# Fused two-layer attention, float32 split in high and low parts: theta written where it is used, only phi copied, and ScalarE's order within a slot

## Chip, cores and metric

The kernel runs on one core of a Trainium2 chip. The metric is the device time of one execution in microseconds (us), the median of the runs.

## What is computed

For each of 32 images x (128 channels by 1024 pixels), two attention layers follow one another:

```
theta = W_theta x + b_theta            # 64 x 1024
phi   = W_phi x + b_phi                # 64 x 1024
x1    = x + W_fuse (x softmax(theta^T phi / 8)^T) + b_fuse
h     = group_norm(x1)
q, k, v = W_q h + b, W_k h + b, W_v h + b
y     = x1 + W_p (v softmax(q^T k / sqrt(128))^T) + b_p
```

All inputs and outputs are float32. To keep float32 precision, the kernel splits an operand into a rounded high part and the rest, the low part, and multiplies the parts separately.

## The kernel before, in words

**Rounds and slots.** The work is a pipeline of rounds, one for each image, and each round has 16 slots. In slot s TensorE makes the scores of tile s (128 queries by 1024 keys): tiles 0 to 7 are layer 1 of the round's own image, tiles 8 to 15 layer 2 of the image before it. The loops over slots are written out in the program (`body`, one in each engine's block), and a hardware loop repeats a round. Every engine works through its own fixed list: within a slot, functions are called in the order in which `body` names them, and an instruction that waits holds up all that stands behind it on the same engine.

**A tile's way.** TensorE writes the scores into one of three parts of `s_ps` in PSUM (`scores`, line 452). VectorE takes the row maximum (`maxima`, L750), ScalarE the exponential (`exponentials`, L649). Of four tiles, the first is "copied" (exponential into `e_copied` in SBUF, high part by ScalarE at L672, low part by GpSimd), two are "crossed" (high part by ScalarE in `pair_hi`, L674, low part by VectorE in `take_lo`, L767) and one is "turned" (TensorE transposes it, L487, in the slot behind its own; ScalarE takes the high part at L659, VectorE the low at L761). Copied and crossed tiles are transposed by DMA (SyncE's queue, L368). TensorE multiplies the transposed tiles with the values (`values`) from six slots later on. Before TensorE writes scores into a part of PSUM again, it waits until the tile that was there has been read; for a crossed tile that is `take_lo`.

**Units.** Small products share the slots: `UNITS` says which is made in which slot (theta and phi of the next image, tp0 and tp1 for the two halves of its pixels, in slots 10 and 12; v0 in slot 14, v1 in slot 2; k0, k1, q0, q1, w0, w1 for layer 2; gn1 and gn2 for the group norm; mx for a bound). TensorE makes the unit behind the slot's scores; ScalarE brings it to one of the buffers of `stage` (`take_unit`); GpSimd splits it into high and low (`split_units`, L889 and L892) a slot or two later. ScalarE waits until the unit that had the stage buffer before has been split.

**Theta and phi.** W_theta and W_phi stand side by side, so tp0 and tp1 have theta in partitions 0 to 63 and phi in 64 to 127. The product of layer 1 wants theta's high part in partitions 0 to 63 of `theta2` and its low part in 64 to 127, and phi's high and low parts, each twice, in both halves of the partitions of `phi2`. Before, GpSimd wrote the two parts to `tp_hl`, and in slot 13 SyncE copied them with four DMAs once all had been split:

```
sp.dma_start(phi2[0:D, :, :].bitcast(F32), phi_hl).then_inc(s_tp_copy, 16)
sp.dma_start(phi2[D:C, :, :].bitcast(F32), phi_hl).then_inc(s_tp_copy, 16)
sp.dma_start(theta2[0:D, :].bitcast(F32), theta_hl[:, 0, :]).then_inc(s_tp_copy, 16)
sp.dma_start(theta2[D:C, :].bitcast(F32), theta_hl[:, 1, :]).then_inc(s_tp_copy, 16)
```

They are lines 425 to 428. At slot 0 of the next round TensorE waits for all four: `pe.wait_ge(s_tp_copy, 16 * TP_COPIES * before(mx_at, it, 0))`.

**ScalarE's slot, before:** `turned_hi`, `exponentials`, `pair_hi`, `take_unit`, `inputs_hi`. **VectorE's slot, before:** `take_bounds`, `maxima`, `normalised`, `take_lo`, `reciprocals`, `bound_to_scale`, `x_maxima`, `statistics`.

Of the kernel before, what the change touches and what calls it, by code (L numbers as in the profile page):

```python
# [7 lines left out]
F32 = mybir.dt.float32  # L8
F32R = mybir.dt.float32r
# [5 lines left out]
C = 128  # L15
# [37 lines left out]

UNITS = {0: "gn1", 1: "gn2", 2: "v1", 4: "k0", 5: "k1", 6: "q0", 7: "w0", 8: "q1", 9: "mx", 10: "tp0", 11: "w1",
         12: "tp1", 14: "v0"}
STAGE = {"v1": 0, "k0": 1, "k1": 0, "q0": 1, "w0": 0, "q1": 1, "tp0": 0, "w1": 1, "tp1": 0, "v0": 1}

SPLIT_LAG = {"v1": 2, "k0": 1, "k1": 1, "q0": 1, "w0": 1, "q1": 1, "tp0": 1, "w1": 1, "tp1": 1, "v0": 1}
STAGES = 2
XR_SLOT = 0  # L60
XS_SLOT = 1
X_MAX_SLOT = 7
MX_SLOT = 9
X_SLOT = 8
X_LO_SLOTS = (9, 11)
H_SLOT = 2
H_LO_SLOTS = (3, 4)
RES_SLOTS = (5, 12)
TP_COPY_SLOT = 13
TP_COPIES = 4  # L70

INS = ["x", "w_theta_t", "w_phi_t", "w_fuse_t", "q_w_t", "k_w_t", "p_w_t", "v_w", "vectors", "ident",
       "group_avg"]
# [7 lines left out]
def attention_pair(nc: bass.Bass, x, w_theta_t, w_phi_t, w_fuse_t, q_w_t, k_w_t, p_w_t, v_w, vectors,  # L81
# [88 lines left out]
    def until_stage_before(it, s):  # L170
# [4 lines left out]
                         if staged_at(p) and STAGE[UNITS[p % SLOTS]] == STAGE[UNITS[s]]), -SLOTS - 1)  # L175
        return value(lambda i: count(staged_at, 0, last(i) + 1), it)

    def place(s):

        return PAIRS - 1 if s % GROUP == COPIED and s // GROUP % 2 else s % GROUP  # L180
# [24 lines left out]
    with ExitStack() as ctx:  # L205
# [30 lines left out]
        h_hi, h_lo = sb("h_hi", [C, N], F16), sb("h_lo", [C, N], F16)  # L236
        theta2 = sb("theta2", [C, N], F32R)
        phi2 = sb("phi2", [C, 2, N], F32R)

        tp_hl = sb("tp_hl", [C, 2, N], F32R)  # L240
        q_hi, q_lo = sb("q_hi", [C, N], F32R), sb("q_lo", [C, N], F32R)
        k_hi, k_lo = sb("k_hi", [C, N], F32R), sb("k_lo", [C, N], F32R)
        v_hi = [sb(f"v_hi{n}", [P, KB, C], F16) for n in range(2)]
# [70 lines left out]
        s_clamped = [sem(f"bound_clamped{n}") for n in range(4)]  # L314
        s_scale = [sem(f"value_scale_ready{n}") for n in range(4)]
        s_den = sem("den_scaled_ready")
        s_tp_copy = sem("theta_phi_copied")
        s_split_hi = sem("unit_split_hi")
        s_split = sem("unit_split")
        s_xhi = sem("x_hi_ready")  # L320
# [21 lines left out]
        @block.sync  # L342
        def _(sp):
            sp.dma_start(xs[:, :], x[0]).then_inc(s_xs, 16)
            for dst, src in LOADS0:
                sp.dma_start(dst, src).then_inc(s_wload0, 16)
            for dst, src in LOADS:
                sp.dma_start(dst, src).then_inc(s_wload, 16)

            def batch(t, b):  # L350
                return t[b] if isinstance(b, int) else t[bass.ds(b, 1)].rearrange("a c n -> c (a n)")

            def transposes(it, s):
                if here(crossed_at, it, s - 2):
                    move(it, s - 2, crossed_at, s_pair)
                for t in [t for t in COPIED_OUT_SLOTS if COPIED_OUT_SLOTS[t] == s]:
                    move(it, t, copied_at, s_copied)

            def move(it, t, kind, ready):
                if not here(kind, it, t):  # L360
                    return
                r = t % GROUP
                sp.wait_ge(ready, before(kind, it, t) + 1)
                sp.sem_inc(s_carrier)

                sp.wait_ge(s_pv, et_free(it, t))
                sp.sem_inc(s_carrier)
                sp.dma_start_transpose(et[:, t // GROUP % 4, r, :, :],  # L368
                                       pair[:, place(t), :, :].rearrange("q a n -> q (a n)")).then_inc(
                                           s_pair_t[place(t)], 16)  # L370

            def reciprocals_out(it, s):
                first = s - REC_LAG
                if not (first % GROUP == 0 and here(tile_at, it, first)):
                    return
                n, g = before(group_at, it, first), first // GROUP % 2
                sp.wait_ge(s_rden, n + 1)
                sp.sem_inc(s_carrier)

                sp.wait_ge(s_rden_row[g], 16 * before(same_group(first), it, first))  # L380
                sp.sem_inc(s_carrier)
                sp.dma_start(rden_dram[g], rden[:, g, :]).then_inc(s_rden_dram[g], 16)

            def reciprocals_in(it, s):
                first = s - REC_LAG - 1
                if not (first % GROUP == 0 and here(tile_at, it, first)):
                    return
                n, g = before(group_at, it, first), first // GROUP % 2
                sp.wait_ge(s_rden_dram[g], 16 * before(same_group(first), it, first) + 16)
                sp.sem_inc(s_carrier)  # L390
                sp.wait_ge(s_taken, or_none(n - 1))
                sp.sem_inc(s_carrier)
                sp.dma_start(rden_row[:, g, :],
                             rden_dram[g].rearrange("q t -> (q t)").partition_broadcast(P)).then_inc(s_rden_row[g], 16)

            def image_loads(it, s):
                if s == XS_SLOT and here(x_at, it, X_SLOT) and it.like != -1:
                    sp.wait_ge(s_xsplit, 2 * before(x_at, it, 0))
                    sp.sem_inc(s_carrier)
                    sp.wait_ge(s_x_max, before(x_at, it, 0))  # L400
                    sp.sem_inc(s_carrier)
                    sp.wait_ge(s_xr, before(xr_at, it, XS_SLOT))
                    sp.sem_inc(s_carrier)
                    sp.dma_start(xs[:, :], batch(x, it.i + 1)).then_inc(s_xs, 16)

            def stores(it, s):
                out = s - Y_LAG - 1
                if not here(out1_at, it, out):
                    return
                half = (out - OUT_LAG + PHASE) // GROUP  # L410
                cols = slice(half * HALF, (half + 1) * HALF)
                sp.wait_ge(s_y, before(out1_at, it, out) + 1)
                sp.sem_inc(s_carrier)
                sp.dma_start(batch(y, it.i - 2)[:, cols], y_sb[:, cols]).then_inc(s_store[half], 16)

            def tp_copies(it, s):
                if s != TP_COPY_SLOT or not here(mx_at, it, MX_SLOT):
                    return
                sp.wait_ge(s_split, before(staged_at, it, s))
                sp.sem_inc(s_carrier)  # L420

                sp.wait_ge(s_scores, before(tile_at, it, PHASE))
                sp.sem_inc(s_carrier)
                theta_hl, phi_hl = (tp_hl[rows, :, :].bitcast(F32) for rows in (slice(0, D), slice(D, C)))
                sp.dma_start(phi2[0:D, :, :].bitcast(F32), phi_hl).then_inc(s_tp_copy, 16)
                sp.dma_start(phi2[D:C, :, :].bitcast(F32), phi_hl).then_inc(s_tp_copy, 16)
                sp.dma_start(theta2[0:D, :].bitcast(F32), theta_hl[:, 0, :]).then_inc(s_tp_copy, 16)  # L427
                sp.dma_start(theta2[D:C, :].bitcast(F32), theta_hl[:, 1, :]).then_inc(s_tp_copy, 16)

            def body(it):  # L430
                for s in range(SLOTS):
                    reciprocals_in(it, s)
                    transposes(it, s)
                    reciprocals_out(it, s)
                    image_loads(it, s)
                    stores(it, s)
                    tp_copies(it, s)

            iterations(sp, body, first=-1)
            for half in range(2):  # L440
                sp.wait_ge(s_store[half], 16 * NB)

        @block.tensor
        def _(pe):
# [7 lines left out]
            def scores(it, s, half):  # L452
                if not here(tile_at, it, s):
                    return
                if half == 0:
# [6 lines left out]
                    if last is not None and turned_at(last):  # L462
                        pe.wait_ge(s_tlo, until_part_before(turned_at, it, s))
                    if s == 0:
                        pe.wait_ge(s_tp_copy, 16 * TP_COPIES * before(mx_at, it, 0))
                    if s == PHASE:
                        pe.wait_ge(s_split, before(staged_at, it, 7))
                    if s == PHASE + GROUP:
# [119 lines left out]
        def _(act):  # L588
# [8 lines left out]
            def take_unit(it, s):  # L597
# [10 lines left out]
                    return  # L608

                act.wait_ge(s_split, until_stage_before(it, s))  # L610
                to = stage[:, STAGE[name], :]
                if name[0] == "v":
                    act.wait_ge(s_scale[0], before(mx_at, it, s))
# [63 lines left out]
            def body(it):  # L677
                for s in range(SLOTS):
                    turned_hi(it, s)
                    exponentials(it, s)  # L680
                    pair_hi(it, s)
                    take_unit(it, s)
                    inputs_hi(it, s)

            body(It(-1, -1, 0))
# [14 lines left out]
        def _(dve):  # L700
# [119 lines left out]
            def x_maxima(it, s):  # L820
                if s != X_MAX_SLOT or not here(x_at, it, X_SLOT):
# [5 lines left out]
                nc.vector.tensor_reduce(x_max[:, :], xs[:, :], AX.X, ALU.max,  # L827
                                        apply_absolute_value=True).then_inc(s_x_max, 1)

            def bound_to_scale(it, s):  # L830
                s = s - 1
                if here(mx_at, it, s):
                    value_scale(0, before(mx_at, it, s) + 1)
# [6 lines left out]
            def body(it):  # L840
                for s in range(SLOTS):
                    take_bounds(it, s)
                    maxima(it, s)
                    normalised(it, s)
                    take_lo(it, s)
                    reciprocals(it, s)
                    bound_to_scale(it, s)
                    x_maxima(it, s)
                    statistics(it, s - 2, 0)
                    statistics(it, s - 1, 1)  # L850
# [27 lines left out]
        def _(pool):  # L878
# [15 lines left out]
            def split_units(it, s):  # L894
# [6 lines left out]
                pool.wait_ge(s_evac, before(taken_at, it, s) + 1)  # L901
                if name[0] == "t":

                    pool.wait_ge(s_tp_copy, 16 * TP_COPIES * or_none(before(mx_at, it, s) - 1))
                    hi, lo = (tp_hl[:, n, half * HALF:(half + 1) * HALF] for n in range(2))
                    hi_read = hi.bitcast(F32)
                elif name[0] in "qk":

# [148 lines left out]
```

## Time and profile before

| what | us |
|---|---|
| median of 3 runs | 1916.14 (1911.53 to 1922.02) |
| the profiled execution's own time | 1910.44 |
| its span, first to last instruction | 1908.6 |
| VectorE, ScalarE, GpSimd busy | 1383.4, 1404.0, 1379.7 |

The page of the profile gives busy times and shares; L numbers are lines of the kernel. PE is TensorE, DVE is VectorE, ACT is ScalarE, POOL is GpSimd, SP is SyncE, and a q behind an engine's name is its sequencer, which issues DMAs. Matmuls overlap one another, so the rows of the timeline start closer together than they are long.

### The profile page before, as it was taken

What the parts mean: (1) busy time and instruction counts of PE and PEld (TensorE: products, weight loads), DVE (VectorE), ACT (ScalarE), POOL (GpSimd) and SP (SyncE); (2) the same over time, 40 slices, a digit from 0 to 9 for tenths busy, and PEclk for the clock granted to TensorE, in tenths of its full rate; (3) what the DMA queues carried; (4) which work ended last, traced back from release to release, by engine and by line L of the source; (5) the groups of instructions that cost most, each with busy time, mean ns of one, the idle gap of its engine ahead of it and who ended that gap; (6) DMA issues with size and microseconds to landing.
All of it is one profiled execution on the core that took longest, in us unless ns stands there. A gap on an engine that the chain in (4) does not pass through costs nothing.

```text
span 1908.6 us, 34400 instructions
## 1 busy us (share of the span) xinstructions
PE 1738.8 (91%) x8970; PEld 1141.4 (60%) x8970; DVE 1383.4 (72%) x1541; ACT 1404.0 (74%) x2088; POOL 1379.7 (72%) x1449
## 2 busy tenths in 40 slices
PE   4699999999999999999999999999999999999996
PEld 3456656666665666656666565666666666656653
DVE  4478777778777778777778777778777777777764
ACT  3378777778777778777778777778777777877764
POOL 3468766778777778776778776778776778876754
PEclk9799999999999999999999999999999999999999
DMA  4588888898988988888988898888888988888874
GB/s 91 117 161 167 173 177 173 173 176 163 179 178 172 176 174 168 179 176 173 179 173 168 178 180 172 184 173 171 173 178 176 187 169 177 168 170 175 173 140 94
DMA packets 861110, 319.89 MB, mean 168 GB/s; under 512 B 823328, under 2 KB 824224, under 8 KB 856992
## 3 DMA queue, kind: packets, MB, share of 16 engines
q1 hardware_dynamic: 861088, 319.64, 84.0%
q8 instruction: 9, 0.15, 0.0%
q14 instruction: 13, 0.11, 0.0%
HBM read 50.86 MB, written 17.04 MB: 36 GB/s over the span
## 4 chain that ended last, share of the span: by engine, by line
PE 42%; issue 14%; DMA 11%; POOL 11%; ACT 9%; SPq 6%; DVE 4%; POOLq 0%; ACTq 0%; DVEq 0%
PE o_ps L449 15%; PE s_ps L449 15%; DMA theta<-tp_hl 10%; PE m_ps L449 6%; PE s_ps L487 6%; SPq L427 3%; ACT s_ps L649 3%; POOL x_lo L892 2%; ACT et L659 2%; DVE den_scaled L779 2%; ACT h_hi L628 2%; ACT e L649 2%; DVE neg_max L750 1%; POOL tp_hl L892 1%; POOL y_sb L996 1%
## 5 line engine op out<-in xcount | busy, mean ns | idle before, releaser
L750 DVE TENSOR_REDUCE neg_max<-s_ps 128x1 f32<-128x1024 f32 x512 | 625.5, 1222 | 226.4 <-PE s_ps L449 222.6
L449 PE MATMUL o_ps<-et,v_hi 128*128 128x512 f16 x2048 | 709.9, 388 | 20.5 <-issue 10.8
L449 PE MATMUL s_ps<-phi,theta 128*128 128x512 f32 x1024 | 343.3, 460 | 108.9 <-DMA theta<-tp_hl 99.7
L449 PE MATMUL o_ps<-et,v_lo 128*128 128x512 f16 x1024 | 396.7, 387 | 0.0
L449 PEld LDWEIGHTS o_ps<-et,v_hi 128*128 128x128 f16 x2048 | 206.5, 101 | 265.7 <-issue 83.3
L767 DVE SCALAR_TENSOR_TENSOR pair<-s_ps,pair 128x1024 f16<-128x1024 f32 x256 | 312.0, 1219 | 38.5 <-ACT pair L674 37.2
L649 ACT ACTIVATE s_ps<-s_ps,neg_max 128x1024 f32<-128x1024 f32 x256 | 278.0, 1086 | 79.5 <-DVE neg_max L750 77.9
L449 PEld LDWEIGHTS s_ps<-phi,theta 128*128 128x128 f32 x1024 | 201.8, 201 | 184.1 <-DMA theta<-tp_hl 102.6
L892 POOL TENSOR_TENSOR pair<-e_copied,pair 128x1024 f16<-128x1024 f32 x128 | 274.2, 2142 | 22.2 <-ACT pair L672 22.2
L761 DVE SCALAR_TENSOR_TENSOR et<-s_ps,et 128x1024 f16<-128x1024 f32 x128 | 156.8, 1225 | 180.0 <-ACT et L659 180.0
L674 ACT ACTIVATE pair<-s_ps 128x1024 f16<-128x1024 f32 x256 | 262.2, 1024 | 17.6
L449 PE MATMUL s_ps<-k_hi,q_hi 128*128 128x512 f32 x512 | 248.6, 486 | 4.5 <-POOL q_lo L892 2.1
L449 PE MATMUL s_ps<-k_hi,q_lo 128*128 128x512 f32 x512 | 202.7, 396 | 0.0
L449 PE MATMUL s_ps<-k_lo,q_hi 128*128 128x512 f32 x512 | 200.8, 392 | 0.0
L659 ACT ACTIVATE et<-s_ps 128x1024 f16<-128x1024 f32 x128 | 131.1, 1024 | 71.8 <-PE s_ps L487 65.4
L649 ACT ACTIVATE e<-s_ps,neg_max 128x1024 f32<-128x1024 f32 x128 | 142.8, 1115 | 48.4 <-DVE neg_max L750 48.2
L487 PE MATMUL s_ps<-ident_sb,e 128*128 128x128 f32 x1024 | 155.0, 301 | 12.1 <-ACT e L649 12.1
L487 PEld LDWEIGHTS s_ps<-ident_sb,e 128*128 128x128 f32 x1024 | 135.5, 159 | 37.9 <-ACT e L649 27.0
L892 POOL TENSOR_TENSOR v_lo<-stage,v_hi 128x512 f16<-128x512 f32 x128 | 148.2, 1158 | 10.7
L649 ACT ACTIVATE e_copied<-s_ps,neg_shifted 128x1024 f32<-128x1024 f32 x128 | 143.0, 1117 | 4.1
L449 PEld LDWEIGHTS o_ps<-et,v_lo 128*128 128x128 f16 x1024 | 102.7, 100 | 71.5 <-issue 5.0
L672 ACT ACTIVATE pair<-e_copied 128x1024 f16<-128x1024 f32 x128 | 135.3, 1057 | 9.2
(130 smaller groups left out, 2849.2 us busy)
## 6 DMA issues: line engine op xcount, KB each, us to landing
phi<-tp_hl SPq DMA_DIRECT2D x64, 512.0 KB, 5.4
rden_row<-rden_dram SPq DMA_DIRECT2D x128, 256.0 KB, 4.5
xs<-in_x SPq DMA_DIRECT2D x32, 512.0 KB, 4.8
theta<-tp_hl SPq DMA_DIRECT2D x64, 256.0 KB, 7.1
out_y<-y_sb SPq DMA_DIRECT2D x64, 256.0 KB, 3.5
et<-pair SPq DMA_TRANSPOSE x384, 4.5
rden_dram<-rden SPq DMA_DIRECT2D x128, 2.0 KB, 2.0
w_f<-in_w_fuse_t SPq DMA_DIRECT2D x1, 64.0 KB, 2.4
```

The costliest lines, as they stand in the source:

```text
L427: sp.dma_start(theta2[0:D, :].bitcast(F32), theta_hl[:, 0, :]).then_inc(s_tp_copy, 16)
L449: mm = pe.matmul(out, lhs_t, rhs, start=start and n == 0, stop=stop and n == len(terms) - 1)
L487: mm = pe.transpose(s_ps[:, part(t), kb * P:(kb + 1) * P], e[:, kb * P:(kb + 1) * P], ident[:, :])
L628: nc.scalar.activation(h_hi[:, :], x1[:, :], ACT.Identity, scale=gn_a[:, 0:1], bias=gn_b[:, 0:1]).then_inc(s_hhi, 1)
L649: nc.scalar.activation(to[:, :], s_ps[:, r, :], ACT.Exp, bias=bias, accum_out=den[:, g, t % GROUP:t % GROUP + 1]).then_inc(s_exp, 1)
L659: nc.scalar.activation(et[:, t // GROUP % 4, TURNED, 0:KB, :], s_ps[:, part(t), :].rearrange("k (b q) -> k b q", b=KB), ACT.Copy, scale=E_ ...
L672: nc.scalar.activation(pair[:, r, 0, :], e_copied[:, :], ACT.Copy).then_inc(s_copied_hi, 1)
L674: nc.scalar.activation(pair[:, r, 0, :], s_ps[:, part(t), :], ACT.Copy, scale=E_SCALE).then_inc(s_pair_hi, 1)
L750: nc.vector.tensor_reduce(neg_max[:, t % 4:t % 4 + 1], s_ps[:, part(t), :], AX.X, ALU.max, negate=True).then_inc(s_max, 1)
L761: nc.vector.scalar_tensor_tensor(out=blocks[:, KB:2 * KB, :], in0=s_ps[:, part(t), :].rearrange("k (b q) -> k b q", b=KB), scalar=E_SCALE, ...
L767: nc.vector.scalar_tensor_tensor(out=pair[:, r, 1, :], in0=s_ps[:, part(t), :], scalar=E_SCALE, in1=pair[:, r, 0, :], op0=ALU.mult, op1=AL ...
L892: nc.gpsimd.tensor_tensor(out, in_, hi, ALU.subtract).then_inc(sem, 1)
```

## The change

- `stage` gets a third buffer, used by tp0 alone; tp1 keeps buffer 0.
- `tp_hl` goes. GpSimd writes theta's high part to `theta2[0:64]` in an instruction of its own (before the high and low parts), and then high and low of all 128 partitions to `phi2`, of which the lower half is theta's and is overwritten by the copy.
- VectorE gets `theta_lo`: staged theta minus its high part, written to `theta2[64:128]`, for tp0 in slot 12 and tp1 in slot 14.
- SyncE copies phi's two parts from the upper to the lower partitions, for tp0 in slot 12 and tp1 in slot 13. The four copies go.
- ScalarE takes the slot's unit between the exponentials and `pair_hi`.

```
-STAGE = {..., "tp0": 0, "w1": 1, "tp1": 0, "v0": 1}
-STAGES = 2
+STAGE = {..., "tp0": 2, "w1": 1, "tp1": 0, "v0": 1}
+STAGES = 3
+THETA_LO_SLOTS = {12: "tp0", 14: "tp1"}
+PHI_SLOTS = {12: "tp0", 13: "tp1"}
@@ sync, in place of tp_copies
+            def phi_copies(it, s):
+                unit = unit_slot(PHI_SLOTS.get(s))
+                if unit is None or not here(tp_at, it, unit):
+                    return
+                half = int(UNITS[unit][-1])
+                cols = slice(half * HALF, (half + 1) * HALF)
+                sp.wait_ge(s_split, before(staged_at, it, unit) + 1)
                 sp.sem_inc(s_carrier)
+                sp.dma_start(phi2[0:D, :, cols].bitcast(F32), phi2[D:C, :, cols].bitcast(F32)).then_inc(s_phi, 16)
@@ tensor, scores
                     if s == 0:
-                        pe.wait_ge(s_tp_copy, 16 * TP_COPIES * before(mx_at, it, 0))
+                        pe.wait_ge(s_phi, 16 * before(tp_at, it, 0))
+                        pe.wait_ge(s_theta_hi, before(tp_at, it, 0))
+                        pe.wait_ge(s_theta_lo, before(tp_at, it, 0))
@@ scalar, take_unit
                 act.wait_ge(s_split, until_stage_before(it, s))
+                if name in ("tp0", "v1"):
+                    act.wait_ge(s_theta_lo, before(tp_at, it, s))
@@ scalar, body
                     exponentials(it, s)
+                    take_unit(it, s)
                     pair_hi(it, s)
-                    take_unit(it, s)
@@ vector, called behind bound_to_scale
+            def theta_lo(it, s):
+                unit = unit_slot(THETA_LO_SLOTS.get(s))
+                if unit is None or not here(tp_at, it, unit):
+                    return
+                name, n = UNITS[unit], before(tp_at, it, unit)
+                half = int(name[-1])
+                cols = slice(half * HALF, (half + 1) * HALF)
+                dve.wait_ge(s_theta_hi, n + 1)
+                nc.vector.tensor_tensor(theta2[D:C, cols], stage[0:D, STAGE[name], :], theta2[0:D, cols].bitcast(F32),
+                                        ALU.subtract).then_inc(s_theta_lo, 1)
@@ gpsimd, split_units
-                    pool.wait_ge(s_tp_copy, 16 * TP_COPIES * or_none(before(mx_at, it, s) - 1))
-                    hi, lo = (tp_hl[:, n, half * HALF:(half + 1) * HALF] for n in range(2))
+                    pool.wait_ge(s_scores, before(tile_at, it, PHASE))
+                    cols = slice(half * HALF, (half + 1) * HALF)
+                    scaled(theta2[0:D, cols], src[0:D, :], 1.0, 1.0, ALU.mult, ALU.mult).then_inc(s_theta_hi, 1)
+                    hi, lo = phi2[:, 0, cols], phi2[:, 1, cols]
```

## Rows read from the trace of the kernel before

**Rows 1.** The page: busy time, share of the span, instructions, for each engine.

```profile
PE 1738.8 (91%) x8970; PEld 1141.4 (60%) x8970; DVE 1383.4 (72%) x1541; ACT 1404.0 (74%) x2088; POOL 1379.7 (72%) x1449
```

**Rows 2.** Waits, whole span: engine line <- releaser: us in total, times, longest.

```profile
PE s_ps L449 <- DMA theta<-tp_hl: 99.7, 31, 8.7
...
ACT stage L616 <- POOL tp_hl L892: 22.4, 14, 2.3
...
PE s_ps L487 <- ACT e L649: 12.1, 30, 1.5
```

**Rows 3.** Timeline of PE: slot 0 of the 2nd and 31st round of layer 1.

```profile
135.37 1.20 PE L449 MATMUL s_ps<-phi,theta 128*128 128x512 f32 x4 [2.65 <-DMA theta<-tp_hl]
...
1792.49 2.05 PE L449 MATMUL s_ps<-phi,theta 128*128 128x512 f32 x4 [2.71 <-DMA theta<-tp_hl]
```

**Rows 4.** By windows, a round each: PE, PEld, DVE, ACT, POOL busy; PEclk; DMA share; GB/s.

```profile
881.00:939.00 58.00, 55.16 (x281) 36.20 (x281) 42.82 (x47) 43.85 (x65) 43.13 (x45) 0.94 0.90 173
...
1053.00:1109.00 56.00, 51.94 (x280) 34.24 (x280) 43.10 (x47) 43.85 (x65) 43.09 (x45) 1.00 0.87 178
```

**Rows 5.** Timeline of PE, v0 in slot 14 to slot 4: start, us, what, [idle before].

```profile
1045.43 0.28 PE L449 MATMUL m_ps<-w_f_hl,x_hi 128*128 128x128 f32 x1
...
1053.10 1.19 PE L449 MATMUL s_ps<-phi,theta 128*128 128x512 f32 x4 [3.37 <-DMA theta<-tp_hl]
...
1054.27 1.07 PE L487 MATMUL s_ps<-ident_sb,e 128*128 128x128 f32 x8
...
1060.92 0.28 PE L449 MATMUL m_ps<-w_f_hl,x_hi 128*128 128x128 f32 x1
1062.14 0.39 PE L449 MATMUL o_ps<-et,v_hi 128*128 128x512 f16 x1 [0.94 <-issue]
...
1067.28 1.04 PE L487 MATMUL s_ps<-ident_sb,e 128*128 128x128 f32 x8
```

**Rows 6.** Timeline of SP's queue, slots 13 to 15.

```profile
1042.98 0.33 SPq L382 DMA_DIRECT2D rden_dram<-rden  x1
...
1046.77 2.50 SPq L428 DMA_DIRECT2D theta<-tp_hl  x1
...
1050.86 8.55 SPq L368 DMA_TRANSPOSE et<-pair  x3
```

**Rows 7.** DMA issues: KB each, median us from issue to landing.

```profile
phi<-tp_hl SPq DMA_DIRECT2D x64, 512.0 KB, 5.4
rden_row<-rden_dram SPq DMA_DIRECT2D x128, 256.0 KB, 4.5
...
out_y<-y_sb SPq DMA_DIRECT2D x64, 256.0 KB, 3.5
```

**Rows 8.** Timeline of POOL, slots 13 and 14: tp1's low, x1's second half.

```profile
1041.11 1.29 POOL L892 TENSOR_TENSOR tp_hl<-stage,tp_hl 128x512 fp32r<-128x512 f32 x1
1044.92 1.27 POOL L986 TENSOR_TENSOR x<-x,xr 128x512 f32<-128x512 f32 x1 [2.53 <-DVE x L804]
```

**Rows 9.** Timeline of DVE, slots 13 to 1 of the next round.

```profile
1041.28 1.13 DVE L779 SCALAR_TENSOR_TENSOR den_scaled<-den,v_scale,e_factors 128x4 f32<-128x4 f32 x1
...
1047.43 0.68 DVE L814 BATCH_NORM_STATS2 stats<-x 128x6 f32<-128x512 f32 x1
...
1057.65 0.21 DVE L779 SCALAR_TENSOR_TENSOR den_scaled<-den,v_scale,e_factors 128x4 f32<-128x4 f32 x1
```

**Rows 10.** Timeline of ACT, slots 14 to 0: high 13, v0, exponential 15.

```profile
1045.23 1.02 ACT L674 ACTIVATE pair<-s_ps 128x1024 f16<-128x1024 f32 x1
1046.15 0.68 ACT L614 ACTIVATE stage<-m_ps,v_scale 128x512 f32<-128x512 f32 x1
...
1050.11 1.11 ACT L649 ACTIVATE e<-s_ps,neg_max 128x1024 f32<-128x1024 f32 x1 [1.12 <-DVE neg_max L750]
```

**Rows 11.** Timeline of ACT, slots 2 to 4: high 1, exponential 3.

```profile
1060.70 1.02 ACT L674 ACTIVATE pair<-s_ps 128x1024 f16<-128x1024 f32 x1
...
1065.83 1.12 ACT L649 ACTIVATE e<-s_ps,neg_max 128x1024 f32<-128x1024 f32 x1 [0.25 <-DVE neg_max L750]
```

More of the change, by code:

```diff
@@ L55 @@
          12: "tp1", 14: "v0"}
-STAGE = {"v1": 0, "k0": 1, "k1": 0, "q0": 1, "w0": 0, "q1": 1, "tp0": 0, "w1": 1, "tp1": 0, "v0": 1}
+STAGE = {"v1": 0, "k0": 1, "k1": 0, "q0": 1, "w0": 0, "q1": 1, "tp0": 2, "w1": 1, "tp1": 0, "v0": 1}
 SPLIT_LAG = {"v1": 2, "k0": 1, "k1": 1, "q0": 1, "w0": 1, "q1": 1, "tp0": 1, "w1": 1, "tp1": 1, "v0": 1}
-STAGES = 2
+STAGES = 3
 XR_SLOT = 0
@@ L62 @@
 X_MAX_SLOT = 7
-MX_SLOT = 9
 X_SLOT = 8
@@ L68 @@
 RES_SLOTS = (5, 12)
-TP_COPY_SLOT = 13
-TP_COPIES = 4
+THETA_LO_SLOTS = {12: "tp0", 14: "tp1"}
+PHI_SLOTS = {12: "tp0", 13: "tp1"}
 INS = ["x", "w_theta_t", "w_phi_t", "w_fuse_t", "q_w_t", "k_w_t", "p_w_t", "v_w", "vectors", "ident",
@@ L176, in until_stage_before, with unit_slot @@
         return value(lambda i: count(staged_at, 0, last(i) + 1), it)
+    def unit_slot(name):
+        return next((s for s, unit in UNITS.items() if unit == name), None)
     def place(s):
@@ L238, in attention_pair @@
         phi2 = sb("phi2", [C, 2, N], F32R)
-        tp_hl = sb("tp_hl", [C, 2, N], F32R)
         q_hi, q_lo = sb("q_hi", [C, N], F32R), sb("q_lo", [C, N], F32R)
@@ L316, in attention_pair @@
         s_den = sem("den_scaled_ready")
-        s_tp_copy = sem("theta_phi_copied")
+        s_theta_hi, s_theta_lo = sem("theta_hi_ready"), sem("theta_lo_ready")
+        s_phi = sem("phi_twice")
         s_split_hi = sem("unit_split_hi")
@@ L414, in stores @@
                 sp.dma_start(batch(y, it.i - 2)[:, cols], y_sb[:, cols]).then_inc(s_store[half], 16)
-            def tp_copies(it, s):
-                if s != TP_COPY_SLOT or not here(mx_at, it, MX_SLOT):
+            def phi_copies(it, s):
+                unit = unit_slot(PHI_SLOTS.get(s))
+                if unit is None or not here(tp_at, it, unit):
                     return
-                sp.wait_ge(s_split, before(staged_at, it, s))
+                half = int(UNITS[unit][-1])
+                cols = slice(half * HALF, (half + 1) * HALF)
+                sp.wait_ge(s_split, before(staged_at, it, unit) + 1)
                 sp.sem_inc(s_carrier)
[L422 to L428, printed above, removed]
+                sp.dma_start(phi2[0:D, :, cols].bitcast(F32), phi2[D:C, :, cols].bitcast(F32)).then_inc(s_phi, 16)
             def body(it):
@@ L436, in body @@
                     stores(it, s)
-                    tp_copies(it, s)
+                    phi_copies(it, s)
             iterations(sp, body, first=-1)
@@ L847, in body @@
                     bound_to_scale(it, s)
+                    theta_lo(it, s)
                     x_maxima(it, s)
```

## Prediction, written before the kernel with the change was timed

> **What bounds the kernel.** The page first: TensorE is busy for 91% of the span, the other three for 72 to 74% [rows 1]. The waits next: the one wait of weight that TensorE has is that for the copies of theta and phi, 99.7 us in 31 times [rows 2]. It stands at slot 0, and from the second round of layer 1 to the 31st there are 29 rounds in 1657.1 us, 57.14 us each [rows 3]. The first wait of the 31 is the longest (8.7 us, while the pipeline fills); the other 30 are 3.0 us each.
>
> The wait costs more than itself. By windows, a round in which the granted clock is 1.00 throughout lasts 56.0 us, and one with 0.94 lasts 58.0 us [rows 4]: behind most of these waits TensorE runs for a while at 1.2 GHz in place of 2.4. The mean round of 57.14 is thus 1.1 us over the one without a drop. In that one TensorE is busy 51.94 us of 56, and the rest is 3.4 us in front of slot 0 and 0.94 us in slot 2 [rows 4, 5]. So TensorE alone would need 51.9 us a round; all that the change can win is 57.1 - 51.9 = 5.2 us.
>
> **Part 1: the copies.** Before, SyncE issues four DMAs behind rden's [rows 6]; the last starts at 1046.77 and TensorE is released at 1053.06, 6.3 us later [rows 5, 6]. Now one copy of 64 partitions, 256 KB, stands there for tp1, and tp0's goes out a slot earlier. The first copy of phi took 5.4 us for 512 KB from issue to landing, and rden_row's 256 KB 4.5 us [rows 7]; I take 4.5, with the bounds 3.5 (y's 256 KB [rows 7]) and 6.3 (what the last of four took). It needs tp1's split: GpSimd ended that at 1042.40 [rows 8], and gets a theta high part of 0.62 us or less in each of the two units (a TENSOR_SCALAR of POOL over half the partitions; the nearest row, gap included, is the 0.7 us between a unit's high and low). Both lie in the 2.53 us that GpSimd idles in front of x1's second half [rows 8], so x1 isn't late. The split ends at 1043.8, the copy goes out at 1043.9 and lands at 1048.4; TensorE is ready at 1049.7 (1053.10 less 3.37) [rows 5]. The wait is gone with 1.3 us to spare, and with it the clock's drop: -3.0 and -1.1 us a round. At 6.3 us the copy would land at 1050.2 and leave 0.5 us of it.
>
> SyncE's queue gives up 4 issues, of which the last alone takes 2.50 us, and gets 2 of some 0.5. The three transposes behind them start at 1050.86 [rows 6] and run to the 0.94 us wait in slot 2 [rows 5]; TensorE comes to that slot 3.4 us earlier, they about as much, since the pair of tile 14 is what they wait for next. I count this as even, bounds 0 and +0.9.
>
> **Part 2: what takes the wait's place at slot 0.** Behind the scores of tile 0 (0.95 us) and gn1 (0.1) TensorE transposes tile 15, which needs its exponential. That starts at 1050.11 and ends, 1.11 and the accumulator's read of 0.2 behind it, at 1051.3 [rows 10]. TensorE would now be there at 1049.73 + 1.05 = 1050.8: 0.5 us short, which the copies hid before. The new order makes it longer. v0's last product ends at 1045.71 [rows 5]; ScalarE has exponential 13 done by 1045.2 and now waits for v0, takes it (0.6 us until the next can start), and starts high 13 at 1046.3 in place of 1045.23 [rows 10]. Low 13 on VectorE follows from 1047.4 to 1048.6, then come the statistics (0.68 us [rows 9], and 0.4 with their aggregate), then the maximum of tile 15, at 1049.6 in place of 1048.77; exponential 15 ends at 1052.2. The stall is 1.4 us. It is the same in the next round, for v0's end is tied to slot 14.
>
> **Part 3: slot 4.** From the transposes of tile 15 to those of tile 3 TensorE takes 13.01 us, 0.94 of it the wait: 12.1, and about 11.9 without the tails [rows 5]. ScalarE's path over the same stretch (high 15, exponentials 0 to 3, their high parts, v1, h's high part) takes 12.8: exponential 3 ends at 1067.0 against 1054.27 [rows 5, 11]. Today it waits 0.15 and 0.25 us in it. v1's last product ends at 1061.20 [rows 5], high 1 started at 1060.70 [rows 11]: taking v1 first puts 0.6 us of idleness in front of it. 12.8 + 0.6 - 0.4 = 13.0, so TensorE waits 1.1 us for exponential 3. In the other slots ScalarE waits for the unit too, but there layer 2's scores are longer (six matmuls to four) and the gap closes; 0.2 us for slot 8. The gain of taking a unit early (GpSimd starts up to 1.1 us sooner, tp1 no longer waits for tp0's split, 22.4 us over the run [rows 2]) meets an engine with time to spare: nothing. Without the cover of GpSimd's idle time the two theta instructions would cost 1.4 us.
>
> **Part 4: theta's low part.** Two TENSOR_TENSORs of 64x512 on VectorE. No row has this form; the statistics read 512 columns in 0.68 us [rows 9], x1's 1.3 us on GpSimd is the upper bound for the work. tp0's falls in front of the maximum of tile 12, which waits for TensorE anyway. tp1's delays the maximum of tile 14 from 1044.8 to 1045.5, still ahead of exponential 14, which now starts behind high 13 at 1047.4. I count 0.
>
> There is one thing in it: a VectorE instruction with two inputs in SBUF gets slow beside GpSimd. L779, four elements, takes 0.21 us where GpSimd idles and 1.13 us beside L892, and it ends at 1042.41, when that ends at 1042.40 [rows 8, 9]. The Trainium skill ("SBUF — State Buffer", section "SBUF: two separate sides") calls this an exclusive lock that either side holds for a whole instruction, so GpSimd too would stand still. theta_lo has two such inputs, so each can wait up to 1.29 us and take 0.7 us from GpSimd. By the row alone VectorE waits and GpSimd doesn't.
>
> **Sum.** 51.9 + 1.4 + 1.1 + 0.2 is 54.6, less 0.1 for the tails that the stalls hide: 54.5 us, 2.6 under 57.14. Over the 31 intervals between slots 0, 81 us; the first long wait gives some 5 us more. 1910.4 - 86 is 1824 us on the profiled execution's own time, which lies 5.7 us below the median: 1830.
>
> **Rivals.**
> A. The new order costs TensorE nothing, as high parts have slack. For it: ScalarE is busy 74% [rows 1]. Against: part 3's path has 0.4 us of idleness in 12.8. Only 0.5 us of stall at slot 0 stays: 52.4 a round, 4.7 x 31 + 5 less: 1765 us. Chance 0.10.
> B. The clock still falls. For: it falls after most waits of 2.7 us; stalls of 1.4 and 1.1 us are new. Against: the round with 0.94 us kept 1.00 [rows 4, 5]. +1.1 us a round: 1864. Chance 0.12.
> C. The change doesn't do what it says: the copy of phi lands late (6.3 us, or GpSimd 1.5 us late with tp1), TensorE still waits 1.5 us at slot 0 in place of the 1.4 of part 2, then waits for its transposes besides, and the clock drops now and then. +1.6 us: 1880. Chance 0.08.
> D. The lock works both ways. tp1's theta_lo meets x1's sum on GpSimd, waits up to 1.3 us, and holds up the maximum of tile 14 until 1046.9 to 1048.1; exponentials 14 and 15 follow 0.7 us later, and so does slot 0. 55.2 a round: 1851. The skill's page named above is what speaks for it. Chance 0.10.
> E. Slower: high parts behind units. Each of the ten units now puts its own 0.6 to 0.78 us and the wait for TensorE's product (0.1 to 0.6) in front of a high part, so of the low part and of the scores three tiles on. If none of the ten had slack, 10 x 0.7 + 2.5 = 9.5 us a round, 61.4: +132 us, 2050. It turns the sign from 5.2 us on, over half of the ten fully exposed; by my parts 2.7 us are. Chance 0.05; 0.05 more that it comes out even (5 us of stalls).
>
> **Numbers.** The forecast keeps 0.50. Within 0.5% (about what a measurement of this kernel can tell from no change) 0.05, slower 0.05, faster 0.90. The forecast's own range is 1800 to 1850 (stalls 1 us smaller or 0.7 larger); with B, D and the nearer halves of A and C the range reaches from 1775 to 1880, and leaves out 0.19.
>
> **What would show it.** Right: no wait for a DMA at slot 0; TensorE's waits now L487 on ACT e L649, some 1.4 us at slot 0 and 1 at slot 4; PEclk 9 or more in all slices; rounds of 54.5 us; stage rows on ScalarE waiting for m_ps at v0 and v1 that didn't before. Wrong: L449 s_ps still released by a DMA (C); PEclk at 0.5 once a round (B); theta_lo over 1.3 us and GpSimd rows of x1 with idle time in front of them (D); waits of L449 s_ps for DVE pair (E).

## The result, and the profile after

The changed kernel takes 1871.99 us (median of 4 runs, 1869.81 to 1875.33) against 1916.43 us of the kernel before: ratio 0.977 (95% interval 0.974 to 0.980), so 44 us or 2.3% faster. The forecast was 1830 us, its own range 1800 to 1850; 1872 lies outside that and inside the wider range up to 1880, into which rival B (the clock still falls) had been counted. The sign and the path of the waits came as forecast; of the 86 us that the sum promised, about half did not come.

The page of the changed kernel, busy times, PEclk and the DMA issue of the new copy:

```profile
span 1873.5 us, 34679 instructions
PE 1715.6 (92%) x8970; PEld 1121.1 (60%) x8970; DVE 1424.0 (76%) x1605; ACT 1392.2 (74%) x2088; POOL 1452.1 (78%) x1513
...
PEclk9799999999999999999999999999999999999999
...
phi<-phi SPq DMA_DIRECT2D x64, 256.0 KB, 3.3
```

VectorE has 41 us more than before (two low parts a round) and GpSimd 72 us [rows 1]. Two waits of the changed kernel, then VectorE's wait for high parts in the kernel before and in this one:

```profile
PE s_ps L487 <- ACT e L652: 98.8, 90, 1.9
...
ACT stage L617 <- PE m_ps L447: 81.4, 64, 3.2
```

```profile
DVE pair L767 <- ACT pair L674: 37.2, 80, 1.4
DVE pair L770 <- ACT pair L677: 203.6, 190, 2.9
```

TensorE's wait for the copies, 99.7 us [rows 2], is gone; in its place it waits 98.8 us for ScalarE's exponentials ahead of its transposes, where it had waited 12.1 us. The second line is ScalarE waiting for v0 and v1, which took 18.4 us in the kernel before. The last two are VectorE waiting for the high part of a crossed tile, which now comes behind a unit: 203.6 us for 37.2.

Slot 0 of the 2nd and 31st round on the timeline of PE, as in [rows 3]:

```profile
133.04 1.27 PE L447 MATMUL s_ps<-phi,theta 128*128 128x512 f32 x4
...
1754.84 0.58 PE L447 MATMUL s_ps<-phi,theta 128*128 128x512 f32 x1
```

That is (1754.84 - 133.04) / 29 = 55.92 us a round, 1.22 less than 57.14. The spans of the two profiled executions differ by 35.1 us: the 29 rounds save 35.3, the start saves 2.3 more, and the end, where the pipeline runs empty, takes 2.6 longer.

By windows, two neighbouring rounds (columns as in [rows 4]), and the two waits of TensorE in the round behind them:

```profile
915.14:970.42 55.28, 52.06 (x282) 34.29 (x281) 43.96 (x49) 43.41 (x66) 45.87 (x48) 1.00 0.82 161
970.42:1027.36 56.94, 53.73 (x282) 34.97 (x281) 44.12 (x49) 43.36 (x66) 45.38 (x48) 0.97 0.78 157
```

```profile
1030.62 1.09 PE L487 MATMUL s_ps<-ident_sb,e 128*128 128x128 f32 x8 [1.86 <-ACT e L652]
...
1043.87 1.09 PE L487 MATMUL s_ps<-ident_sb,e 128*128 128x128 f32 x8 [1.16 <-ACT e L652]
```

A round is 52.06 us of TensorE and 3.2 us of stalls: 1.86 in slot 0, 1.16 in slot 4, 0.2 in slot 8. In 18 of the 29 rounds the clock stays at 2.4 GHz and the round lasts 55.3 us; in 11 it falls to 1.2 GHz once, and the round lasts 56.9. (Below, a fall is a round whose granted clock is 0.97 in place of 1.00.) The second of the two rounds above again, with its stall in slot 0 and in three windows:

```profile
973.67 1.30 PE L487 MATMUL s_ps<-ident_sb,e 128*128 128x128 f32 x8 [1.85 <-ACT e L652]
```

```profile
970.42:974.40 3.98, 2.13 (x15) 1.84 (x14) 3.54 (x4) 1.55 (x4) 1.06 (x4) 1.00 1.05 199
974.40:977.81 3.41, 3.41 (x12) 1.75 (x11) 1.68 (x4) 2.41 (x4) 1.06 (x1) 0.50 1.10 205
977.81:1027.36 49.55, 48.19 (x260) 31.38 (x259) 38.90 (x43) 39.40 (x58) 43.25 (x44) 1.00 0.74 150
```

The clock falls 0.7 us behind the end of slot 0's stall and is back before slot 4. So it is in all 11 rounds: the fall begins 0.7 to 1.4 us behind the end of slot 0's stall, and none follows slot 4's.

The way to the 1.86 us, first on ScalarE (v0, high 13, exponential 14, exponential 15):

```profile
1023.90 0.69 ACT L617 ACTIVATE stage<-m_ps,v_scale 128x512 f32<-128x512 f32 x1 [1.42 <-PE m_ps L447]
1024.48 1.01 ACT L677 ACTIVATE pair<-s_ps 128x1024 f16<-128x1024 f32 x1
1025.39 1.09 ACT L652 ACTIVATE s_ps<-s_ps,neg_max 128x1024 f32<-128x1024 f32 x1
...
1029.36 1.11 ACT L652 ACTIVATE e<-s_ps,neg_max 128x1024 f32<-128x1024 f32 x1 [1.70 <-DVE neg_max L753]
```

and on VectorE (tp1's low part, maximum 14, low 13, statistics, maximum 15):

```profile
1022.24 0.69 DVE L841 TENSOR_TENSOR theta<-stage,theta 64x512 fp32r<-64x512 f32 x1
1022.96 1.23 DVE L753 TENSOR_REDUCE neg_max<-s_ps 128x1 f32<-128x1024 f32 x1
1025.53 1.23 DVE L770 SCALAR_TENSOR_TENSOR pair<-s_ps,pair 128x1024 f16<-128x1024 f32 x1 [1.35 <-ACT pair L677]
1026.67 0.68 DVE L817 BATCH_NORM_STATS2 stats<-x 128x6 f32<-128x512 f32 x1
...
1028.02 1.23 DVE L753 TENSOR_REDUCE neg_max<-s_ps 128x1 f32<-128x1024 f32 x1 [0.29 <-issue]
```

ScalarE idles 1.42 us until TensorE has finished v0; VectorE idles 1.35 us for high 13; ScalarE then idles 1.70 us for maximum 15, and TensorE 1.86 us for exponential 15. That is one wait handed round three engines, from TensorE's v0 back to TensorE. The low part of theta lies in front of it, and behind it VectorE is idle.

### The profile page after: what moved, and what is told of

Its sections match the earlier page's. It is cut to its first block, busy times and chain, and to the rows that moved or that the text cites. A ratio compares the mean times of both kernels' runs of the same rounds, so it can differ in the third digit from the quotient of the medians.

```text
span 1873.5 us, 34679 instructions
## 1 busy us (share of the span) xinstructions
PE 1715.6 (92%) x8970; PEld 1121.1 (60%) x8970; DVE 1424.0 (76%) x1605; ACT 1392.2 (74%) x2088; POOL 1452.1 (78%) x1513
## 4 chain that ended last, share of the span: by engine, by line
PE 57%; issue 18%; ACT 12%; DVE 7%; POOL 1%; ACTq 1%; DMA 1%; SPq 1%; DVEq 0%; POOLq 0%
PE o_ps L447 21%; PE s_ps L447 20%; PE m_ps L447 9%; PE s_ps L487 7%; ACT pair L677 5%; DVE neg_max L753 4%; ACT s_ps L652 2%; ACT h_hi L631 2%; DVE x_max L830 2%; ACT pair L675 2%; ACT e L652 1%; DVE stats L817 1%; DMA et<-pair 1%; SPq L370 1%; DVE pair L770 0%
## 5 line engine op out<-in xcount | busy, mean ns | idle before, releaser
L770 DVE SCALAR_TENSOR_TENSOR pair<-s_ps,pair 128x1024 f16<-128x1024 f32 x256 | 312.9, 1222 | 203.8 <-ACT pair L677 203.6
L447 PEld LDWEIGHTS s_ps<-phi,theta 128*128 128x128 f32 x1024 | 203.6, 200 | 79.0 <-issue 6.4
L487 PE MATMUL s_ps<-ident_sb,e 128*128 128x128 f32 x1024 | 138.9, 279 | 99.0 <-ACT e L652 98.8
L487 PEld LDWEIGHTS s_ps<-ident_sb,e 128*128 128x128 f32 x1024 | 113.0, 141 | 137.9 <-ACT e L652 133.4
L1004 POOL TENSOR_TENSOR x<-x,xr 128x512 f32<-128x512 f32 x64 | 96.9, 1514 | 64.4 <-DVE x L807 64.4
```

Source lines behind the costliest of these rows:

```text
L447: mm = pe.matmul(out, lhs_t, rhs, start=start and n == 0, stop=stop and n == len(terms) - 1)
L487: mm = pe.transpose(s_ps[:, part(t), kb * P:(kb + 1) * P], e[:, kb * P:(kb + 1) * P], ident[:, :])
L770: nc.vector.scalar_tensor_tensor(out=pair[:, r, 1, :], in0=s_ps[:, part(t), :], scalar=E_SCALE, in1=pair[:, r, 0, :], op0=ALU.mult, op1=AL ...
L1004: nc.gpsimd.tensor_tensor(x1[:, cols], x1[:, cols], xr[:, cols], ALU.add).then_inc(s_x1, 1)
```

## Experiments

The rounds below are taken like those above, from the first matmul of slot 0 in the 2nd and in the 31st round; they compare the kernels better than medians do: the median of the kernel before lay between 1904 and 1916 us in these measurements, and each ratio is to the one taken beside it.

**The order back, theta in place kept.** In ScalarE's `body`:

```
                     exponentials(it, s)
-                    take_unit(it, s)
                     pair_hi(it, s)
+                    take_unit(it, s)
```

> The change with ScalarE's old order in all slots (high part, then unit); theta and phi as in the change. Theory: the new order makes most of the two stalls that the changed kernel shows (1.85 us in slot 0, 1.16 us in slot 4). Without it slot 0 keeps some 0.6 us and slot 4 some 0.5, and no stall is long enough for the clock to fall: rounds of 53.2 us in place of 55.9, 1872 - 31 x 2.7 = 1790 us. Rival 1 (theta's low part and the lock with GpSimd make the stalls): both stay, 1872. Rival 2 (the early unit is what gained): above 1872.

Measured: 1774.78 us, ratio 0.929 (0.925 to 0.932); rounds of 52.86 us ((1658.35 - 125.36) / 29). TensorE waits 25.6 us for ScalarE's exponentials in place of 98.8. In slot 0 the stall is 0.28 to 0.67 us, most often 0.36. One round's waits:

```profile
973.47 1.09 PE L487 MATMUL s_ps<-ident_sb,e 128*128 128x128 f32 x8 [0.64 <-ACT e L652]
...
985.95 1.09 PE L487 MATMUL s_ps<-ident_sb,e 128*128 128x128 f32 x8 [0.17 <-ACT e L652]
```

The clock falls in none of the 29 rounds. So the first half of the change alone is worth 7.1%, and the second half gives two thirds of it back: 97 us between the medians. What of the 7.1% theta in place brings, and what the single copy of phi, no run separates.

**The new order alone**, in the kernel before (the two lines exchanged there).

> The kernel before with the new order alone. Theory: slot 0's longer way is hidden behind the copies, slot 4's stall grows from some 0.2 to 1.1 us: rounds of 58.0 us, 1916 + 28 = 1944 us. Rival 2 (the early unit gains): below 1911. If the order is of no weight by itself: 1916.

Measured: 1943.74 us, ratio 1.018 (1.014 to 1.023), rounds of 58.14 us. Its waits in one round:

```profile
1009.16 2.08 PE L449 MATMUL s_ps<-phi,theta 128*128 128x512 f32 x4 [3.08 <-DMA theta<-tp_hl]
...
1025.00 1.09 PE L487 MATMUL s_ps<-ident_sb,e 128*128 128x128 f32 x8 [1.08 <-ACT e L649]
```

Slot 0 shows only the copies, slot 4 the 1.08 us. The order is a loss with either way of writing theta. The copies hid its larger part. The clock falls in all 29 rounds there.

**Only v0 behind the high part; only v1 behind it.** The edit, with (14,) or (2,) for the slots:

```
+                    if s in (14,):
+                        pair_hi(it, s)
                     take_unit(it, s)
-                    pair_hi(it, s)
+                    if s not in (14,):
+                        pair_hi(it, s)
```

> The change, but in slot 14 alone ScalarE makes high 13 ahead of v0. Theory: slot 0's stall of 1.85 us falls by 1.1 us (wait for v0 and its 0.6 us gone from the way to exponential 15), slot 4's stays at 1.16, and the clock no longer falls: 55.9 - 1.1 - 0.6 = 54.2 us a round, 1819 us. Rival 1: 1.85 us stays, 1872.

> The change, but in slot 2 alone ScalarE makes high 1 ahead of v1. Theory: slot 4's stall of 1.16 us falls by 0.7 or more, slot 0's stays at 1.85, and the clock falls as often as now: 55.2 us a round, 1850 us. If the clock's falls need both stalls, they go too: 1832 us. Rival 1: 1872.

Measured: 1819.17 us (ratio 0.952, 0.948 to 0.955) with v0 behind and 1827.29 us (0.956, 0.953 to 0.960) with v1 behind. The waits of one round, v0 behind:

```profile
945.77 1.09 PE L487 MATMUL s_ps<-ident_sb,e 128*128 128x128 f32 x8 [0.84 <-ACT e L652]
959.01 1.09 PE L487 MATMUL s_ps<-ident_sb,e 128*128 128x128 f32 x8 [1.16 <-ACT e L652]
```

and v1 behind:

```profile
947.25 1.09 PE L487 MATMUL s_ps<-ident_sb,e 128*128 128x128 f32 x8 [1.85 <-ACT e L652]
959.73 1.09 PE L487 MATMUL s_ps<-ident_sb,e 128*128 128x128 f32 x8 [0.39 <-ACT e L652]
...
973.21 1.09 PE L487 MATMUL s_ps<-ident_sb,e 128*128 128x128 f32 x8 [0.20 <-ACT e L652]
```

Each edit takes its own stall: v0's place makes 1.0 us of slot 0's, v1's 0.77 us of slot 4's. V1's leaves slot 0's as it was; with v0 behind, slot 4's is often shorter too (0.44 to 1.17 us in 26 rounds, median 0.96). With either edit nearly all falls of the clock end (none and one in 29 rounds), though slot 0 still stalls 1.85 us in the second.

**Both behind, the eight others ahead** (slots (2, 14) in the same edit).

> The change, but in slots 2 and 14 ScalarE makes the high part ahead of v1 and v0; the eight other units stay ahead of the high part. Theory: these two carry all that the new order costs, since only there a high part that waits for TensorE's twelve-matmul unit leads to the next wait of TensorE; rounds of 52.8 us as with the old order in all slots, 1775 us. Rival: the other units add up as well, each some tenths: 1790 us or more. If the early units gain something where they are ready: 1765.

Measured: 1797.58 us, ratio 0.943 (0.940 to 0.946), rounds of 53.62 us. The theory was wrong here: 0.76 us a round over the order back in all slots. Slot 0 keeps 0.84 us, where the old order has 0.36:

```profile
987.38 1.09 PE L487 MATMUL s_ps<-ident_sb,e 128*128 128x128 f32 x8 [0.84 <-ACT e L652]
```

**Only theta's and phi's units and w1 ahead** (slots 10, 11 and 12), which tells where that 0.76 us is; **the old order once more** beside it.

> The change, but only tp0, w1 and tp1 (slots 10 to 12) are taken ahead of the high part. Theory: GpSimd has idle time, so taking theta's units early gains nothing, and three high parts come 0.7 to 1.1 us later, of which TensorE sees little: ratio 0.929 to 0.935. Rival 2 (that is where an early unit pays): below 0.925. If these three are the 0.8 us a round that eight early units cost: 0.943.

> The old order in all slots with theta in place once more, five rounds, beside the other three on one chip: ratio 0.929 to the kernel before, 52.9 us a round.

Measured: 1796.48 us, ratio 0.944 (0.941 to 0.946), against 1775.9 us, ratio 0.933 (0.930 to 0.936), for the order back. 53.47 us a round against 52.94: 0.53 us, most of the 0.76 if such parts can be added. They cannot quite: slot 0's stall is longer here than with all eight ahead, 1.1 us as a rule and up to 1.49:

```profile
984.90 1.09 PE L487 MATMUL s_ps<-ident_sb,e 128*128 128x128 f32 x8 [1.49 <-ACT e L652]
```

Even the units that the new order was best placed to help cost 1.2% by being early. Which of the three it is, and how a late high part reaches slot 0 from there, was not followed further.

**Tp1's low part made twice, in the changed kernel.** Ahead of `theta_lo`'s instruction:

```
+                if half == 1:
+                    dve.wait_ge(s_again, before(tp1_at, it, unit))
+                    nc.vector.tensor_tensor(again[D:C, :], stage[0:D, STAGE[name], :],
+                                            theta2[0:D, cols].bitcast(F32), ALU.subtract).then_inc(s_again, 1)
```

> The change, with tp1's low part of theta made twice on VectorE in slot 14 (the first time into a tile of its own; 0.7 us more on VectorE a round). Theory: in the changed kernel the maximum of tile 14 behind it has 1.1 us to spare, since exponential 14 waits behind the late high 13: 1872. Rival (theta's low part and the lock are on the way to slot 0): 0.7 us a round more, 1894.

Measured: 1906.12 us, ratio 1.001 (0.999 to 1.002), 34 us over the change by the medians and 1.22 us a round. And **the same with the old order**:

> ScalarE's old order in all slots, and tp1's low part made twice as in the run before. Theory: here nothing stands between it and the way to exponential 15, so 0.7 us a round come on top: 1775 + 31 x 0.7 = 1797 us. If the low part isn't on the way: 1775.

Measured: 1826.2 us, ratio 0.959 (0.956 to 0.963), 51 us over the order back. Both came out dearer than expected, because the second instruction takes far more than 0.7 us. VectorE and then GpSimd in the second of the two kernels:

```profile
993.63 0.68 DVE L848 TENSOR_TENSOR again<-stage,theta 64x512 fp32r<-64x512 f32 x1
994.24 1.76 DVE L850 TENSOR_TENSOR theta<-stage,theta 64x512 fp32r<-64x512 f32 x1
996.03 1.23 DVE L758 TENSOR_REDUCE neg_max<-s_ps 128x1 f32<-128x1024 f32 x1
```

```profile
993.68 1.77 POOL L1013 TENSOR_TENSOR x<-x,xr 128x512 f32<-128x512 f32 x1 [0.29 <-DVE x L812]
995.41 2.60 POOL L916 TENSOR_TENSOR pair<-e_copied,pair 128x1024 f16<-128x1024 f32 x1
```

The first low part starts at 993.63; GpSimd's sum of x1 starts beside it and takes 1.77 us in place of 1.27; the second low part takes 1.76 us in place of 0.69 and ends at 996.00, and GpSimd's next instruction takes 2.60 us in place of 2.14. So, by these durations, one stands still while the other runs. Maximum 14 starts 2.40 us behind the first of the two, where it starts 0.72 us behind a single low part (1022.24 to 1022.96 above): the doubling costs VectorE 1.7 us, not 0.7. With that price the places in the theory hold. In the changed kernel some 1.1 us of it are spare (maximum 14 ends at 1024.19 and exponential 14 starts at 1025.39), and a round without a fall of the clock takes 55.95 us for 55.28. With the old order nothing is spare, and slot 0's stall goes from 0.36 us, the commonest there, to 2.03; a round without a fall takes 54.18 us for 52.86. The rest is the clock, which falls in 21 and in 7 of the 29 rounds. What a single low part costs, the next two runs tell.

**Theta's low part shrunk to 8 columns** from the second image on (the rest of it keeps the first image's values), in the changed kernel and with the old order:

```
+                some = HALF if it.like < 0 else 8
+                cols = slice(half * HALF, half * HALF + some)
-                nc.vector.tensor_tensor(theta2[D:C, cols], stage[0:D, STAGE[name], :], ...
+                nc.vector.tensor_tensor(theta2[D:C, cols], stage[0:D, STAGE[name], 0:some], ...
```

> The change, with theta's low part written over 8 columns of 512 from the second image on (that part of the computation is left out, as in the run with the old order). Theory: in the changed kernel the low part isn't on the way (maximum 14 has 1.1 us to spare), and what it takes from GpSimd by the lock (0.5 us twice a round) is idle time there: slot 0 keeps its 1.85 us, ratio 0.977 to the kernel before as for the change. Rival (it makes part of the 1.85 us): the stall falls to 1.4 us or less and the clock no longer falls: ratio 0.965.

> ScalarE's old order in all slots, and theta's low part written over 8 columns of 512 from the second image on (the rest of it keeps the first image's values, so this part of the computation is left out). Theory: with the old order the low part of tp1 stands on the way to exponential 15 (maximum 14, low 13, statistics, maximum 15 follow it without a gap); without its 0.7 us slot 0's stall of 0.4 to 0.6 us goes: 52.3 us a round, 1760 us. If it costs nothing there: 1775.

Measured: 1867.47 us (ratio 0.981, 0.979 to 0.984) in the changed kernel, rounds of 55.90 us against 55.92, and the same two stalls:

```profile
970.03 1.10 PE L487 MATMUL s_ps<-ident_sb,e 128*128 128x128 f32 x8 [1.85 <-ACT e L652]
984.94 1.09 PE L487 MATMUL s_ps<-ident_sb,e 128*128 128x128 f32 x8 [1.16 <-ACT e L652]
```

With the old order 1766.25 us (0.927, 0.925 to 0.930), 52.52 us a round against 52.86 and 52.94; slot 0's stall is 0.28 us in every round. The low part is free in the changed kernel, and costs some 0.4 us a round once the high parts are in time; by the medians (1766 against 1775 and 1776) half a per cent. GpSimd, whose own work is the same, is busy 1418.9 us with the shrunk low parts in the changed kernel, against 1452.1: 33 of its 72 us more are time in which VectorE's low parts held it up.

**Two stage buffers, old order.** STAGE of tp0 back to 0, STAGES to 2, and ScalarE's wait for `s_theta_lo` also ahead of tp1.

> ScalarE's old order, theta in place, but two stage buffers as before: tp0 in the one that tp1 takes, and ScalarE waits for tp0's low part before it takes tp1. Theory: GpSimd and VectorE are done with tp0 within 0.5 us of the time when ScalarE would take tp1, so the third buffer is worth 0 to 0.5 us a round: ratio 0.929 to 0.937. Rival (the third buffer is needed for the gain): 0.945 or more.

Measured: 1779.75 us, ratio 0.936 (0.933 to 0.938), beside 1775.9 us and 0.933 (0.930 to 0.936) with three; 52.93 and 52.94 us a round. The third buffer is worth nothing in a steady round, and at most the 4 us (0.2%) between the medians, which the intervals do not tell from nothing.

## Why the forecast came out as it did

**Part 1 held.** The copy of phi takes 3.3 us from issue to landing (4.5 forecast), and no row of TensorE at slot 0 waits for a DMA, so rival C falls too. TensorE alone needs 52.06 us a round, 51.94 in the kernel before [rows 4]. With the old order the two halves of the gain, the wait and the clock, came in full: 57.14 to 52.86.

**Part 2 held in kind and was too small.** From the end of v0's last product (1023.71) to the transposes of tile 15 (1030.62) it takes 6.91 us, against 6.5 forecast; TensorE's own work in between is 5.05 us (5.1). ScalarE starts v0 0.19 us behind the product's end, which the sum left out, and VectorE needs another 0.2 up to maximum 15. The stall is 1.86 us for 1.4. The idle time that the new order puts on ScalarE in front of v0 is larger than the 0.5 us read from the rows of before: 1.42, since exponential 13 ends 1.23 us ahead of v0's last product. It didn't matter: the way starts at v0's end, not at ScalarE's wait. The runs with v0 behind and with v1 behind show which unit makes which stall. They show the stall of slot 0 made up otherwise than in the forecast, which had 0.5 us without the new order and 0.9 for v0: it is 0.36 without the new order, 0.5 from the early units of other slots (0.84 against 0.36), and 1.0 for v0.

**Part 3 held:** 1.16 us for 1.1, and 0.2 us in slot 8. The kernel before with the new order gave 58.14 us a round for 58.0 expected.

**The step that failed is the clock.** The sum gave back all the falls (1.1 us a round); rival B stood beside it as all or nothing. What came is 11 falls in 29 rounds at 1.66 us each (56.94 - 55.28): 0.63 us a round. With 0.46 from slot 0, 0.16 from TensorE's own time (52.06 for 51.9), 0.06 from slot 4, and the 0.1 that was taken off for tails, that makes up the 1.42 us between 54.5 and 55.92. Over 29 rounds this is 41 us. That the distance from 1830 to 1872 is 42 is partly luck. On the profiled executions the forecast was 1824 us and the time 1875.33, 51 us apart: the other 10 us are the start and the end (5 us for the first long wait and two more rounds' gain were forecast, and nothing in sum came). The profiled execution lay 5.7 us below the median before and 3.3 us above it after, which takes 9 us off again. The error of slot 0 may have counted twice: with 2.32 us in place of 1.85 there (the low part made twice) 21 rounds fall in place of 11. No run holds the forecast's 1.4 us beside slot 4's 1.16; the one round of the change that has 1.40, its first, keeps the clock.

**Part 4, and rival D.** The mechanism of D is there: GpSimd stands still as well, as the doubled instruction shows, and as the Trainium skill ("SBUF — State Buffer", section "SBUF: two separate sides") says with its exclusive lock; the row of L779 alone had shown only VectorE's side. In the changed kernel the two low parts take 0.95 and 0.69 us, and GpSimd's neighbours 1.06 and 1.77 us in place of 0.62 and 1.27; by the shrunk low part that is 33 us of GpSimd's time over the run. The price that D put on it was wrong: zero there, by the shrunk low part. The forecast's 0 for part 4 was right because maximum 14 had time to spare behind the late high 13.

**Rivals A and E.** A (the order costs nothing) falls with 97 us. E had the right cause and too high a price: two of the ten units carry most of it. That three others (tp0, w1, tp1) cost 0.5 us a round by themselves was not in any part of the forecast; part 3 had counted them at nothing.

## What to carry to other kernels

An engine that takes its work in a fixed order should not be made to wait for a product that has just been started while it holds an operand that others need: here 1.4 us of such waiting went round ScalarE, VectorE and back to TensorE. Two edits of one change want two predictions and two runs: one half was worth 7.1%, the other took back 4.8 points of it. And when a long wait is removed, look for the shorter ones that stood in its shadow: each is priced from the moment at which its chain starts, and the clock may answer to what is left of them.

## What the runs showed of the hardware

TensorE's clock and the stalls in front of the transposes, falls counted over 29 rounds (where one number stands, it is the commonest):

| kernel | stall in slot 0 | in slot 4 | falls | round, us |
|---|---|---|---|---|
| old order | 0.28 to 0.67 | up to 0.42 | 0 | 52.86 |
| old order, once more | 0.28 to 0.67 | up to 0.42 | 1 | 52.94 |
| v0 behind | 0.28 to 0.88 | up to 1.17 | 0 | 54.26 |
| v1 behind | 1.85 | 0.39 | 1 | 54.57 |
| old order, low part twice | 2.03 | 0.23 to 0.4 | 7 | 54.65 |
| the change | 1.85 | 1.16 | 11 | 55.92 |
| the change, low part shrunk | 1.85 | 1.15 | 11 | 55.90 |
| the change, low part twice | 2.32 | 1.17 | 21 | 57.14 |

With a stall of 1.85 us and little behind it the clock fell once in 29 rounds; with the same and 1.16 us in slot 4, 13 us later, in more than a third of them. That the second stall is the cause isn't shown, and the traces speak against the simplest form of it: in the four kernels that stall 1.85 us or more in slot 0 and fall more than once, every fall begins between 0.2 us ahead of the end of slot 0's stall and 1.4 us behind it, never behind slot 4's. Stalls of 1.85 or 1.86 us are followed by a fall in 11 rounds of the change and by none in 16 others. And each edit that takes a stall away also changes the length of the round (54.5 us for 55.3), and so the times at which slot 0's stall recurs. Whether the falls follow those times or the second stall is left open. Once a fall came behind a lone, shorter wait: the one fall of the old order when measured once more begins 0.3 us behind the end of a wait of 1.36 us, 8 us behind slot 0's of 0.39. Each fall lasts some 3.4 us at 1.2 GHz in the records and costs 1.5 to 2.0 us, 1.7 in the change.

Two instructions of 64 partitions and 512 columns: GpSimd's copy takes 0.61 us, as that of 128 partitions does (0.62), and VectorE's subtraction with both inputs in SBUF 0.69 us when GpSimd doesn't hold it up.

The version that the experiments point to, theta in place with ScalarE's old order, beats both kernels: 1774.78 and 1775.9 us when measured twice, ratios 0.929 and 0.933.
